# Expert pairs on TensorE's column halves, keys moved into their loop, and a second attention begun by halves

## The reference, cut to what matters

```python
# layer 0, feed-forward: 32 experts, 4 per token, capacity 40, over T = 1024 tokens
Xp = x[slots_token].reshape(E, C, d)                  # 32 x 40 x 256
G = jnp.einsum('ecd,edi->eci', Xp, W_gate)            # 256 -> 128
U = jnp.einsum('ecd,edi->eci', Xp, W_up)
Y = jnp.einsum('eci,eid->ecd', jax.nn.silu(G) * U, W_down)
out = jnp.zeros((T, d)).at[slots_token].add(Y.reshape(EC, d) * slots_w[:, None])
x = x + jnp.tanh(g_ffn[0]) * (out + shared)
# layer 1, attention: 16 heads of 16, 1024 queries and keys, int8-like rounding
q = (layernorm(x) @ Wq + bq) * scale;  k, v = split(ctx @ Wkv + bkv)
q, k = _fq_sym(q, axis=-1), _fq_sym(k, axis=-1)       # scale = max|.| / 127, round
v = _fq_sym(v, axis=2)
attn = _fq_unsigned(softmax(q @ k.T))                 # max / 255, round
x = x + jnp.tanh(g_xattn[1]) * (attn @ v @ Wp + bp)
```

## Time and profile before

| what | us |
|---|---|
| median of three runs (lowest, highest) | 933.48 (928.96, 934.51) |
| the profiled execution | 931.75 |
| its span, first to last instruction | 929.7 |
| TensorE busy | 714.6 (77%) |
| VectorE busy | 552.0 (59%) |
| ScalarE busy | 371.5 (40%) |
| GpSimd busy | 347.5 (37%) |

### The profile page before, as it was taken

The page is one execution under the profiler, slowest core; times in us unless marked ns, Lnnn a source line. Parts: engine busy times, 40 slices in busy tenths (PEclk is TensorE's granted clock), DMA queues, the critical chain, the costliest instruction groups (busy, mean ns, idle before and its releaser), DMA issues.

```text
span 929.7 us, 14328 instructions
## 1 busy us (share of the span) xinstructions
PE 714.6 (77%) x5159; PEld 497.0 (53%) x5204; DVE 552.0 (59%) x1276; ACT 371.5 (40%) x673; POOL 347.5 (37%) x365
## 2 busy tenths in 40 slices
PE   4986799993558777777788795196586549999997
PEld 2434454563435555555664684154255427678776
DVE  3797847338779999999548453755696650000004
ACT  4002023212479989898621232233374303221220
POOL 3741220463317767676401732440141044000124
PEclk9997899997778889898789998598697759999999
DMA  6311117896009999999920475500004123415413
GB/s 223 131 58 47 32 44 210 220 127 61 1 19 171 187 161 182 168 175 164 185 85 13 136 141 182 169 9 0 1 1 182 45 56 114 153 57 198 149 47 118
DMA packets 139218, 102.78 MB, mean 111 GB/s; under 512 B 109714, under 2 KB 124300, under 8 KB 137102
## 3 DMA queue, kind: packets, MB, share of 16 engines
q1 hardware_dynamic: 130472, 79.10, 35.0%
q0 software_dynamic: 7760, 22.16, 11.6%
q10 hardware_dynamic: 918, 0.62, 0.2%
HBM read 65.34 MB, written 11.33 MB: 82 GB/s over the span
## 4 chain that ended last, share of the span: by engine, by line
PE 40%; DVE 23%; issue 17%; ACT 7%; DMA 7%; POOL 5%; POOLq 0%; DVEq 0%; SPq 0%; ACTq 0%
PE psum L2290 7%; PE psum L2309 5%; DMA both<-moe_y_dram,moe_idx_from 3%; PE psum L1608 3%; ACT both L1292 3%; DVE xnT L1399 2%; PE psum L214 2%; DVE both L329 2%; PE psum L818 2%; DVE both L333 2%; POOL both L561 2%; DVE xn L171 2%; PE psum L1208 2%; PE psum L1885 2%; PE psum L1623 1%
## 5 line engine op out<-in xcount | busy, mean ns | idle before, releaser
L1399 DVE TENSOR_SCALAR_CACHE_REDUCE xnT<-psum,both 128x1024 bf16<-128x1024 f32 x128 | 157.6, 1282 | 15.3 <-PE psum L1208 14.9
L1119 POOL TENSOR_SCALAR both<-both 128x1024 f16<-128x1024 f32 x128 | 133.7, 1044 | 82.8 <-ACT both L1292 74.4
L1292 ACT ACTIVATE both<-psum,both 128x1024 f32<-128x1024 f32 x128 | 153.5, 1209 | 14.0 <-DVE xnT L1399 13.7
L1208 PE MATMUL psum<-both 128*128 128x512 bf16 x215 | 76.9, 429 | 40.7 <-ACT both L1292 33.8
L2290 PE MATMUL psum<-both 128*128 128x320 f32 x256 | 75.0, 448 | 3.9 <-ACT both L549 3.9
L1229 PEld LDWEIGHTS psum<-both 128*128 128x128 f16 x1024 | 64.2, 99 | 25.6 <-issue 12.7
L1229 PE MATMUL psum<-both 128*128 128x16 f16 x1024 | 68.5, 172 | 9.0 <-DVE xn L1408 6.9
L561 POOL DMA_INDIRECT both<-moe_y_dram,moe_idx_from x48 | 46.8, 975 | 73.8 <-DMA moe_y_dram<-both 48.8
L2369 ACT ACTIVATE both<-psum 128x320 f32<-128x320 f32 x64 | 27.7, 437 | 111.5 <-PE psum L2290 93.6
L1230 PE MATMUL psum<-both,minus_base 128*128 128x16 f16 x1024 | 67.0, 171 | 0.0
L1230 PEld LDWEIGHTS psum<-both,minus_base 128*128 128x128 f16 x1024 | 59.3, 99 | 12.3 <-issue 4.6
(11 more groups left out here) (379 smaller groups left out, 1508.0 us busy)
## 6 DMA issues: line engine op xcount, KB each, us to landing
both<-in_l_experts SPq DMA_DIRECT2D x50, 384.0 KB, 3.8
both<-in_l_experts SPq DMA_DIRECT2D x16, 1024.0 KB, 5.5
grouped_y_dram<-both SPq DMA_DIRECT2D x31, 128.0 KB
ctok<-in_ctx SPq DMA_DIRECT2D x2, 1024.0 KB, 8.2
both<-kpad_dram SPq DMA_DIRECT2D x1, 2048.0 KB, 8.1
moe_xn_dram<-xn POOLq DMA_DIRECT2D x4, 512.0 KB, 4.1
moe_y_dram<-both POOLq DMA_DIRECT2D x7, 256.0 KB, 2.5
both<-both SPq DMA_TRANSPOSE x96, 3.7
```

The costliest lines, as they stand in the source:

```text
L1119: nc.gpsimd.tensor_scalar(r2[n % RSLOTS2], e2[:, n % ESLOTS2, :], 255.0, HALF_BASE, ALU.mult, ALU.add).then_inc(sem("r2_ready"), 1)
L1208: last = nc.tensor.matmul(bank[2 * (n % SRING2) + half], qz2[:, h % 2, h // 2, t * P:(t + 1) * P], kT2[:, h // 2, half * 512:(half + 1) * ...
L1292: nc.scalar.activation(e2[:, n % ESLOTS2, :], scores_at(n), ACT.Exp, bias=bias2[:, n:n + 1], scale=s2[:, t * H2 + h:t * H2 + h + 1], accum ...
L1399: nc.vector.tensor_scalar(scaled2[n % 2], scores_at(n), ns2[:, t * H2 + h:t * H2 + h + 1], None, ALU.mult, ALU.min, accum_out=bias2[:, n:n ...
```

## The change

Layer 0's experts go in pairs: two experts' 40 rows lie at partitions 0 and 64 of one bank, written by matmuls into the column halves of TensorE, and silu, product, turn and copies run once per pair over 104 partitions. Twelve experts are gathered instead of 15, stored in two pieces of two DMAs; 20 are own, in seven blocks. Zeros that the memsets on VectorE wrote are written by GpSimd; rows 32 to 63 of two banks are filled by ScalarE. Key projection and scales go before the loop, two products of the rounding to GpSimd, the casts and subtractions and the values' scaling into the loop. The second attention evicts the values first, projects queries by halves, copies whole pairs in turn on two engines, has no clears and contracts scores over 48 rows. A group's sums are turned at units 35 and 36 and it is scaled out in front of unit 39.

```diff
-        L0, GE0 = 3 * C0, 15
+        L0, GE0 = 3 * C0, 12
+        PAIRS0, GP0 = E0 // 2, GE0 // 2
+        HALF = P // 2
+        PAIR0 = HALF + C0
-        Y0_STORES = (0, 7, 13, GE0)
+        Y0_STORES = (0, 3, GP0)
+        OWN_ADDS0 = 26
+        ADDED0 = {10: 1, 11: 5, 12: 8, 13: 11, 14: 15, 15: 18, 16: 21}
+        def down0_count(e):
+            return e // 2 + 1 if e < GE0 else GP0 + e - GE0 + 1
...
             for e in range(RING0, E0):
-                sp.wait_ge(sem("block_down_done"), e - RING0 + 1)
+                sp.wait_ge(sem("block_down_done"), down0_count(e - RING0))
...
             moe0.load_rows_gpsimd(pool)
+            nc.gpsimd.memset(exp_h, 0.0).then_inc(sem("small_consts"), 1)
+            nc.gpsimd.memset(hz_words, 0.0).then_inc(sem("small_consts"), 1)
+            keys_gpsimd(pool)
             moe0.gather_gpsimd(pool)
...
             l1x_keys_tensor(pe)
+            pe.wait_ge(sem("vf2_ready"), 4)
...
+            def up(p):
+                for e in (2 * p, 2 * p + 1):
+                    pe.wait_ge(sem(f"ring_loaded{e % RING0}"), (e // RING0 + 1) * 16)
...
+                if p >= 2:
+                    pe.wait_ge(sem("block_h_ready"), p - 1)
                 for c in range(DC):
+                    for m in range(2):
+                        e = 2 * p + m
...
+                        last = nc.tensor.matmul(bank[p % 2][m * HALF:m * HALF + C0, 0:2 * P].rearrange("p (j n) -> p j n", j=2),
+                                                moe0.rowsT[:, c, e * C0:(e + 1) * C0], w[:, :, c, :], start=(c == 0), stop=(c == DC - 1))
...
+            def down_gathered(p):
...
+                for m in range(2):
+                    last = nc.tensor.matmul(bank[3][m * HALF:m * HALF + C0, 0:D], exp_hT[:, p % 2, m * HALF:m * HALF + C0],
+                                            down_weights(2 * p + m), start=True, stop=True)
...
+            for s in range(PAIRS0 + 3):
+                if s < PAIRS0:
+                    up(s)
+                if s >= 3 and opens_block_inside_pair(2 * (s - 3) + 1):
+                    down_own(2 * (s - 3) + 1)
+                for b in range(GB0, BLOCKS0):
+                    if last_pair(b) + 3 == s:
+                        own_rows(b)
+                if 1 <= s <= PAIRS0:
+                    turn(s - 1)
+                if 0 <= s - 2 < GP0:
+                    down_gathered(s - 2)
+                elif GP0 <= s - 2 < PAIRS0:
+                    down_own(2 * (s - 2))
+                    if not opens_block_inside_pair(2 * (s - 2) + 1):
+                        down_own(2 * (s - 2) + 1)
...
+            copy_keys = {8: lambda: keys_scalar(act, 0), 11: lambda: keys_scalar(act, 1)}
...
-            l1x_values_vector(dve, seq)
-            seq.step(nc.vector.memset(exp_h, 0.0))
-            seq.step(nc.vector.memset(exp_hz, 0.0))
+            seq.step(nc.vector.tensor_reduce(sv2[:], vT2, AX.X, ALU.max, apply_absolute_value=True))
+            keys_begin_vector(dve, seq)
...
+            between = {3: lambda: own(0), 5: lambda: own(1), 7: lambda: own(2), 9: lambda: own(3), 11: lambda: own(4), 14: lambda: own(5),
+                       15: lambda: own(6)}
+            between.update(values_steps(dve, seq))
...
+            added = add_until(OWN_ADDS0, added)
+            moe0.wait(dve, "added", added)
+            own_add(0)
+            own_add(1)
             seq.wait()
+            tile_stats(seq, range(NT // 2))
+            own_add(2)
+            own_add(3)
+            ln_begin(dve, seq, 2, 0)
+            added = add_until(OWN_ADDS0 + 2, added)
+            ln_finish(dve, seq, 2, 0)
...
-            nc.gpsimd.memset(qz2_words[ROWS:P, 0], 0.0).then_inc(sem("pads2_ready"), 1)
-            nc.gpsimd.memset(qz2_words[0:ROWS, 1], 0.0).then_inc(sem("pads2_ready"), 1)
+        def keys_gpsimd(pool):
+            pool.wait_ge(sem("keys_steps"), 1)
+            times2(nc.gpsimd, kf2, isk2).then_inc(sem("keys_steps"), 1)
+            pool.wait_ge(sem("keys_steps"), 3)
+            times2(nc.gpsimd, kf2, sk2).then_inc(sem("kd2_ready"), 1)
...
+            def turn_q_or_keys_before_half_1():
+                pe.wait_ge(sem("ka2_ready"), 1)
+                turn_pairs(range(4))
+                project(0)
...
+            pe.wait_ge(sem("v2_ready"), 2)
+            ln_tensor(pe, 2, turn_q_or_keys_before_half_1)
+            project(1)
+            turn_pairs(range(4, H2 // 2))
             pe.wait_ge(sem("qa2_ready"), 2)
+            turn_pairs(range(H2 // 2, H2))
...
+                of_head = slice(h % 2 * ROWS, h % 2 * ROWS + 3 * HD2)
                 for half in range(2):
-                    last = nc.tensor.matmul(bank[2 * (n % SRING2) + half], qz2[:, h % 2, h // 2, t * P:(t + 1) * P],
-                                            kT2[:, h // 2, half * 512:(half + 1) * 512], start=True, stop=True)
+                    last = nc.tensor.matmul(bank[2 * (n % SRING2) + half], qT2[of_head, h // 2, t * P:(t + 1) * P],
+                                            kT2[of_head, h // 2, half * 512:(half + 1) * 512], start=True, stop=True)
...
+            root(0)
+            evacuate_T(act, xnT, sem("xnT_blocks"), sem("xnT_ready"), turned(2), 0)
+            root(1)
+            copy_pairs(range(4))
+            evacuate_T(act, xnT, sem("xnT_blocks"), sem("xnT_ready"), turned(2), 1)
+            copy_pairs(range(4, H2))
...
+            return {1: scales, 2: lambda: scaled(0), 6: lambda: scaled(1),
+                    8: lambda: nc.vector.tensor_scalar(vi2, vT2, MAGIC, None, ALU.subtract).then_inc(sem("vi2_ready"), 1)}
...
+            return {4: rounded, 10: lambda: part(0).then_inc(sem("kd2_ready"), 1), 12: lambda: seq.step(nc.vector.memset(ka[:, :, 3 * HD2:ROWS], 0.0)),
+                    13: lambda: part(1).then_inc(sem("ka2_ready"), 1)}
...
             for n in range(U):
-                past = n - LAG2 - 1
-                if past > 0 and past % (GH2 * NT) == 0:
-                    scale_out(past // (GH2 * NT) - 1)
+                group, at = n // (GH2 * NT) - 1, n % (GH2 * NT)
+                if group >= 0 and at == SUMS2:
+                    sums_times(group)
+                if group >= 0 and at == SUMS2 + 1:
+                    sums_turned(group)
+                if group >= 0 and at == LAG2:
+                    scale_out(group)
                 top(n)
```

More of the change, by code:

```diff
@@ L871, in l0f_scalar @@
             l1x_values_scalar(act)
+            act.wait_ge(sem("small_consts"), 3)
+            act.wait_ge(sem("vf2_ready"), 4)
+            for i in range(2):
+                nc.scalar.copy(bank[i][P // 4:HALF, 0:2 * P], bp2[P // 4:HALF, :])
             for g in range(len(moe0.groups)):
@@ L990, in l0f_vector, with add_until @@
-            tile_stats(seq, range(added // K0))
-            while added < NT * K0:
-                add(added)
-                added += 1
-                if added % K0 == 0:
-                    moe0.wait(dve, "added", added)
-                    tile_stats(seq, (added // K0 - 1,))
-                if added in keys_end:
-                    keys_end[added]()
+            def add_until(n, added):
+                while added < n:
+                    add(added)
+                    added += 1
+                return added
@@ L1134, in l1x_turn_sync, with pair_by_vector, pairs_before @@
               .then_inc(sem(f"rT2_ready{n % RSLOTS2}"), 16)
+        def pair_by_vector(n):
+            return n >= H2 // 2 and n % 2 == 1
+        def pairs_before(n, by_vector):
+            return sum(pair_by_vector(m) == by_vector for m in range(n))
         def pair_copied(eng, n):
-            eng.wait_ge(sem("qkT2_ready"), n + 1)
-            if n >= H2 // 2:
-                eng.wait_ge(sem("qT2_ready"), n + 1 - H2 // 2)
+            if pair_by_vector(n):
+                eng.wait_ge(sem("qT2_ready"), pairs_before(n + 1, True))
+            else:
+                eng.wait_ge(sem("qkT2_ready"), pairs_before(n + 1, False))
         def l1x_values_tensor(pe):
@@ L1161, in l1x_tensor, with project, turn_pairs @@
         def l1x_tensor(pe):
-            def project(first, src, w, halves=False):
-                for t in range(NT):
-                    if halves and t % 4 == 0:
-                        pe.wait_ge(sem("xnT_ready"), 8 + t // 2 + 2)
+            def project(half):
+                pe.wait_ge(sem("xnT_ready"), 8 + 2 * half + 2)
+                for t in range(4 * half, 4 * half + 4):
                     for c in range(DC):
-                        last = nc.tensor.matmul(bank[first + t // 2][:, t % 2 * D:(t % 2 + 1) * D], src[:, c, t * P:(t + 1) * P],
-                                                w[:, c, :], start=(c == 0), stop=(c == DC - 1))
+                        last = nc.tensor.matmul(bank[t // 2][:, t % 2 * D:(t % 2 + 1) * D], xnT[:, c, t * P:(t + 1) * P],
+                                                wq2[:, c, :], start=(c == 0), stop=(c == DC - 1))
                     if t % 2:
```

(5 more changed lines are left out.)

301 lines of the change are left out of this document (148 added, 153 removed).

## The result

| what | before | after |
|---|---|---|
| median of four runs (lowest, highest) | 934.0 (928.96, 935.25) | 949.0 (948.19, 950.18) |
| ratio to before, 95% interval | | 1.0185 (1.0136 to 1.0234) |
| span of the profiled execution | 929.7 | 947.0 |
| granted clock, mean | 0.882 | 0.790 |
| TensorE busy | 714.6 | 781.2 |

What follows compares the result with a forecast made beforehand. Bounds: TensorE in the expert loop, then y gathers, then engines one after another; VectorE and ScalarE in attention. Wins of 4.4 + 13 + 3.6 = 21 off 931.75 gave 911, own range 904 to 918.

Steps and rivals of the forecast that it cites:

- 0.73 + 0.10: Attention loop: TensorE's busy share plus one change of form per unit for 48-row scores; stays hidden, taken as 0 us.
- Rival 4: Attention loop: scores become the bound if 48-row pieces cost over 0.36 a unit; each further 0.1 costs 12.8 us; chance 0.07.
- The last add: Behind the expert loop: last add to x starts at 227 against 231.35, 4.4 won.
- I get the end of the last own block at 216: Expert loop: last own block ends at 216 (205 to 222 depending on load landings), against 213.9 before.
- by the row not at all: Expert loop's start: weighting own experts wouldn't wait for GpSimd's first product; by the skill's rule pairs would begin 3 us later.
- 0.92 + 0.13: Pair loop: a pair's up product takes 0.92 for 8 records, plus 0.13 for a change of the array's form.
- The waits for ring loads: Pair loop: TensorE waits some 2.3 each in iterations 4 and 6, some 2, 7 and 5 in 12 to 14.
- The gathers: Expert loop: last store issued at 153.8, landing 4.2 later, so gathers of y rows start at about 158 instead of 170.09.
- rival 1: Pair loop: the ring starves, loads land in 12, last block ends at 228; time 923; chance 0.18.
- From the last add to the first scores: Stretch before attention: 40.1 becomes about 27 through no clears, halved query projection and copies on two engines; 13 won.
- The loop's other edits: Attention loop: scaling groups out one unit sooner and moving sums gain 1.2 at each of three places, 3.6 in all.
- rival 3: Pair loop: column halves don't overlap with 40 weight columns, an iteration takes 3.3; time 917; chance 0.05.

Runs made afterwards that it cites:

- mixed: The changed kernel with every second unit's scores over all 128 rows, the others over 48; 935.2.
- rows128: The changed kernel with scores contracting over all 128 rows of a pair, so each is the sum of two heads' scores; 914.6, ratio 0.9808.
- before48: The kernel before with only the scores changed, to contract over 48 rows; 974.7.
- rows64: The changed kernel with scores over 64 rows instead of 48; 953.7.
- extra: The changed kernel with one more 512-column product over all 128 rows per unit, overwritten by the 48-row one; 1005.8.
- rowpairs: The changed kernel with a unit's two score halves taken from different row halves, rows 0 to 47 and 64 to 111; 916.2.
- halves128: The changed kernel with scores over all 128 rows, each product in two column halves of 64 queries; 913.1.
- masked_nolock: The changed kernel, scores over 128 rows with the other head's query rows zeroed, GpSimd's first keys product begun behind the own experts' weighting; 914.9, ratio 0.9802.
- lag1: As masked_nolock, with a pair's down product one iteration sooner, own pairs and spreading likewise; 906.1, ratio 0.9698.
- tinyloads: As masked_nolock, but the 24 expert-weight loads inside the loop bring 32 bytes per partition instead of 3072; 900.2.

## Why the prediction was wrong

**The step that failed** is in the attention loop: "TensorE, 33.05 busy of 45, goes to 0.73 + 0.10: it stays hidden ... I take 0". Both numbers are shares of the 1.355 that a unit took. The 0.10 stands for one change of form, 0.13 us; mixed shows two of 0.10 at 1.2 GHz, 0.20 us or 0.15 of a unit. That term was too small, but with it alone TensorE would still have been hidden. What failed is the 0.73. It held at a clock of 0.91, and the text carried that clock over to a loop with another kind of product. At 0.50 a unit takes 1.28 and a quarter of a turn's 0.83, some 1.49 by estimate, without any change of form (1.28 from rows128, 0.83 from after), and 1.68 on average with them (213.5 / 127), so TensorE becomes the bound. Rival 4 had place and sign, and its sign in the profile (pitch above 1.36 with TensorE busy) is what came. It named the clock of 0.91, but took it as given, was priced on changes of form alone, and got 0.07.

The Trainium skill (TensorE: Matmul & The Clock Gate, What's actually happening) says that the clock is set by how busy TensorE has been of late. By that rule a TensorE that is busy 50.00 of 50.00 runs at 2.4 GHz; here it stayed at 0.50 through some 210 us, and the measurement decides. Why it stayed there is open. All loops with products over part of the rows had 0.50 (after, before48, rows64, extra, mixed, and rowpairs with two row halves at once); those with column halves or with rows of zeros had 0.86 to 1.00 (halves128, masked_nolock). In every run that has them, few rows at work and the array's form for a part of its rows go together, so the runs don't tell which of the two it is.

**The last add** came 2.9 later instead of 4.4 sooner. Three terms of "I get the end of the last own block at 216" were off:
- "by the row not at all": the weighting of own experts took 3.83 beside GpSimd's product (0.39 without it), and the third pair's up product began 5.7 behind the first one's (2.1 in masked_nolock). The Trainium skill (GPSIMD Engine Reference, Specifications) says that GpSimd contends with VectorE's instructions of two SBUF inputs too; weighed there and put aside for one row beside a clear, the rule held beside a product, with these numbers. It set little more than the start: without it masked_nolock ends the loop 1 sooner.
- "0.92 + 0.13" for a pair's up product is what it took at full clock, 1.06. But the clock in the three stretches was 0.82 to 0.90, where it had been 1.00 from 136 to 213.9 before, and seven of sixteen pairs took 1.9. All up products together are 22.9 busy instead of 16.8, and TensorE's work in the loop is 67.7 instead of 59.
- The waits for ring loads add up to 17.0, against 18.6 forecast, so their sum was right, if not their places: 3.3 in iteration 9, 6.5 in 13 and little in 12 and 14. What the 216 lacked is 8.7 more of work, most of it from the lower clock (61.7 in lag1 at 0.96), and 4.8 of other waits, 3.3 of them from the late start, where the sum had left 2.9.

The gathers began at 169.31 instead of 158: the last store was issued at 162.10 instead of 153.8, and 7.2 passed from there to the first gather, not 4.2; why the store took longer no run shows. The end of the last block, 224.9, lies nearer to rival 1's 228 than to the 216, but not by rival 1's mechanism, which had the waits grow.

The tail behind the last block was 9.3 (forecast 11).

**From the last add to the first scores**: 25.0 against 27 forecast and 40.1 before. Right: no clears, normalizing in 1.38 instead of 6.85, halves projected beside VectorE's work. The second half was done 17.8 behind the last add (251.00 and 0.96; forecast 18 to 21), and copies and first scores took 7.2 (forecast 7.5).

**The loop's other edits**: 3.6 forecast, 4.6 measured (181.2 to 176.6 in rows128), with no gap at the group. **Column halves overlap**: eight records in 1.06, so rival 3 was rightly low.

The sum with the measured terms: 2.9 lost, 15.1 and 4.6 won, 931.75 - 16.8 = 915; rows128, which undoes the failed step alone, took 914.6. That they agree to 0.4 is luck, since its runs lie between 909.6 and 916.5.

## What to carry to other kernels

Idle time of TensorE is measured at a granted clock: before an edit is called hidden, compute the stage at 1.2 GHz too, and ask whether the new product keeps the clock up (here rows padded with zeros did, part rows in turn with full ones did not). In a ring of buffers, count the iterations between the release of a slot and its next use before halving them; giving each slot back one iteration sooner was worth about 9 here, together with the higher clock that came with it.

## What was not expected of the hardware

- Products over 48 or 64 rows in turn with full ones went with a granted clock of 0.50 for some 210 us, with TensorE busy 48 to 50 of 50; one more full-row product of 512 columns per unit didn't raise it, and neither did two row halves at once.
- Products into row halves overlap: 0.54 for two of 512 columns at 1.2 GHz, against 0.96 in one row half.
- A VectorE step of 128x2 numbers took 2.43 and ended with the GpSimd product of two inputs beside it; a product of VectorE's with one input in PSUM took its 0.29 in the same stretch of masked_nolock (137.36).
- While gathers ran, loads of 4 KB landed 6.4 after their issue (tinyloads, issued in 172:190), as late as the median of the 384 KB loads in after (6.4, issued in 172:200; the longest 12.9).
